# A four-layer graph network on one core: clears on GpSimd behind each gather of the third layer

## The chip, the cores and the metric

The kernel runs on one of the cores of a Trainium2 chip. A core has five engines that run side by side: TensorE (PE in the profile), VectorE (DVE), ScalarE (ACT), GpSimd (POOL) and SyncE (SP). Engines wait for each other through counters, the semaphores. The metric is the device time of one execution in microseconds, the median of three runs: 18546.07 us, with runs from 18542.13 to 18560.46 us. The profile is that of a further execution, taken by the hardware profiler.

## The reference

A graph of 12,500 nodes with 32 features each and 400,000 edges goes through four layers, each followed by a sum with its input and a layer norm:

```
x = layernorm(x + L0(x, edge_attr_3))      # Gaussian weights per edge, sum by node, 32x32 product
x = layernorm(x + L1(x, edge_weight, ...)) # tensor product per edge, sum by node
x = layernorm(x + L2(x, edge_attr_32))     # the third layer, below
x = layernorm(x + L3(x, src, dst))         # ten rounds of a normalised sum by node
```

The third layer, which the change touches, is

```
e_feat = concatenate([x[src], x[dst], edge_attr], axis=-1)   # 96 numbers per edge
h = relu(e_feat @ W1 + b1)                                   # 64
v = h @ W2 + b2                                              # 32
x_cand = segment_max(v, dst)                                 # maximum by node
out = maximum(x_cand, x)
```

## The kernel before, in words

The edges are sorted by their target node and cut into G = 196 groups of 2048 edges (128 partitions x T = 16). Each layer is a stage of its own, with a program for each engine. In the profile the first layer runs from about 630 to 6,550 us, the second from 6,600 to 12,430, the third from 12,915 to 17,820, the fourth from 18,000 to the end.

The third layer's program starts at line 2450. For each group its engines do this:

- **POOL** (function `gathers`, lines 2527 to 2539) fetches the source rows x[src]. One gather is an indirect DMA (line 2537): it takes 128 row numbers from `s_i`, one for each partition, and brings 128 rows of 32 words from the table `d_tab` into one slot of `xg[n]`. A group is 16 such gathers (CH x ST = 4 x 4), one behind the other. There are DEEP = 4 buffers `xg`, used in turn, so POOL may be up to four groups ahead. Before a group it waits for `fxg{n}` (line 2532), the word that buffer n has been read; behind the wait stands the wait's decrement (line 2533, under which the profile books the idle time). At a group that begins a block of four, it also waits for the row numbers (`li{d}`, loaded by SP).
- **PE** waits in `features` (line 2671) until all 16 gathers of the group have landed (`gx{n}`), turns them into `xp` by four transposes (line 2674) and says so on semaphore `xp`.
- **ACT** waits for that (line 2620) and copies `xp` to `XT` (line 2621).
- **PE**, in `step` (line 2685), waits for `XT` (line 2691), frees the gathers' buffer by `fxg` (line 2692) and multiplies `XT` and `U` by W1 into `hb` (lines 2695 and 2696). ACT applies the ReLU (line 2616), PE multiplies by W2 into `vp` (line 2681), DVE takes the running maximum by node (`scan`, line 1180), PE turns the result back (line 1195), ACT copies it and stores it.
- **DVE** also makes `U`, the targets' rows and edge features spread over their edges (line 2574).

Between these, the engines do a share of the fourth layer's preparation: DVE makes one-hot rows (`ol`, line 1021, and `ok`, line 1023), PE multiplies them (`pw`, line 1035), ACT stores the result (line 1050). Nothing plans the order at run time: each engine's program is written out, one block of eight groups as the body of a loop, and only semaphores hold one engine against another. POOL has nothing else to do in this stage than the 196 x 16 = 3136 gathers.

Of the kernel before, what the change touches and what calls it, by code (L numbers as in the profile page):

```python
# [20 lines left out]
P = 128  # L21
# [3 lines left out]
T = 16  # L25
GE = T * P
EP = G * GE
ST = 4
# [124 lines left out]
def gnn_kernel(nc, a, out):  # L153
# [7 lines left out]
    def S(name):  # L161
        if name not in sems:
            keep = name.startswith(lasting)
            sems[name] = spare.pop() if spare and not keep else ctx.enter_context(nc.semaphore(f"{name}_{next(serial)}"))
        return sems[name]
# [15 lines left out]
    def sb(stack, name, shape, dt=F32):  # L181
        made[0] += 1
        return stack.enter_context(nc.sbuf_tensor(f"{name}_{made[0]}", shape, dt))
# [41 lines left out]
    with ctx:  # L225
# [42 lines left out]
        with ExitStack() as st, nc.Block() as block:  # L268
# [7 lines left out]
            @block.sync  # L276
            def _(e):
                e.dma_start(dA[:, :], a["dst_f"][1:EP + 1].rearrange("(p m) -> p m", p=P)).then_inc(S("ld"), 16)
                e.dma_start(dB[:, :], a["dst_f"][0:EP].rearrange("(p m) -> p m", p=P)).then_inc(S("ld"), 16)
                e.dma_start(d_srcf.rearrange("(p m) -> p m", p=P), a["src_f"].rearrange("(p m) -> p m", p=P)  # L280
                            ).then_inc(S("cp"), 16)
                e.dma_start(d_dstf[0:EP].rearrange("(p m) -> p m", p=P), a["dst_f"][0:EP].rearrange("(p m) -> p m", p=P)
                            ).then_inc(S("cp"), 16)
                e.dma_start(d_dstf[EP:EP + 1].rearrange("(a m) -> a m", a=1),
                            a["dst_f"][EP:EP + 1].rearrange("(a m) -> a m", a=1)).then_inc(S("cp"), 16)
                e.wait_ge(S("cp"), 48)
                e.sem_inc(S("cp"), -48)
# [573 lines left out]

        early.close()
        KR = -(-max(k for _, _, k in RUNS) // 2)
        PU = 4
        HEADS = ((0, 2), (2, 8), (8, WPC))
# [105 lines left out]
        def count_buffers(st, runs):  # L971
            kmax = max(n for _, _, n in runs)
            A = {}
            A["iotak"] = sb(st, "iotak", [P, KW], F16)
            A["iotal"] = sb(st, "iotal", [P, P], BF16)
            A["kt"] = [sb(st, f"kt{h}", [P, 3, WPC // 2 * kmax]) for h in range(2)]
            A["ol"] = [sb(st, f"ol{r}", [P, -(-kmax // 2), P], BF16) for r in range(RU)]
            A["ok"] = [sb(st, f"ok{r}", [P, -(-kmax // 2), KW], BF16) for r in range(RU)]
            A["stage"] = [sb(st, f"stage{h}", [P, NB, AC // 8], U16) for h in range(2)]
            return A  # L980
# [4 lines left out]
        def count_start(e, A):  # L985
            if e.engine.name == "Pool":
                e.iota(A["iotak"][:, :], pattern=[[1, KW]], base=0, channel_multiplier=0,
                       allow_small_or_imprecise_dtypes=True)
                e.iota(A["iotal"][:, :], pattern=[[1, P]], base=0, channel_multiplier=0,
                       allow_small_or_imprecise_dtypes=True).then_inc(S("n_iota"), 1)  # L990
            if e.engine.name == "DVE":
                e.wait_ge(S("n_iota"), 1)
                e.sem_inc(S("n_iota"), -1)
            if e.engine.name == "Activation":
                for h in range(2):
                    prime(e, S(f"n_sg{h}"))
                    e.sem_inc(S(f"n_fkt{h}"), 1)
                for r in range(RU):
                    e.sem_inc(S(f"n_fo{r}"), 1)
                e.sem_inc(S("n_fpw"), 2)  # L1000
# [274 lines left out]
        with ExitStack() as st:  # L1275
# [32 lines left out]
            edges = ExitStack()  # L1308
# [586 lines left out]
        with ExitStack() as st:  # L1895
# [24 lines left out]
            edges = ExitStack()  # L1920
# [502 lines left out]
        with ExitStack() as st:  # L2423
# [4 lines left out]
            edges = ExitStack()  # L2428
            st.enter_context(edges)
            s_i = [sb(edges, f"s_i{d}", [P, 4 * T], I32) for d in range(2)]  # L2430
            xg = [sb(edges, f"xg{n}", [P, T, F]) for n in range(DEEP)]
            XT = sb(edges, "XT", [P, SW])
            Wa = sb(edges, "Wa", [P, P])
            ef = [sb(edges, f"ef{d}", [P, 4 * CH, 2, P]) for d in range(2)]
# [15 lines left out]
            with nc.Block() as block:  # L2450
# [70 lines left out]
                @block.gpsimd  # L2521
                def _(e):
                    count_start(e, A)
                    for n in range(DEEP):
                        e.sem_inc(S(f"fxg{n}"), 1)

                    def gathers(r):
                        n, d, w = r % 4, r // 4, r % 4
                        if w == 0:
                            e.wait_ge(S(f"li{d}"), 16)  # L2530
                            e.sem_inc(S(f"li{d}"), -16)
                        e.wait_ge(S(f"fxg{n}"), 1)
                        e.sem_inc(S(f"fxg{n}"), -1)
                        for j in range(CH):
                            for c in range(ST):
                                col = c * T + w * CH + j
                                e.indirect_dma_start(out=xg[n][:, j * ST + c, :], out_offset=None, in_=d_tab,  # L2537
                                                     in_offset=bass.IndirectOffsetOnAxis(ap=s_i[d][:, col:col + 1], axis=0)
                                                     ).then_inc(S(f"gx{n}"), 16)

                    for r in range(4):
                        gathers(r)
                    with e.Fori(0, G // 8) as it:
                        for r in range(8):
                            gathers((r + 4) % 8)
                    for n in range(DEEP):
                        e.wait_ge(S(f"fxg{n}"), 1)
                        e.sem_inc(S(f"fxg{n}"), -1)
                        e.wait_ge(S(f"gx{n}"), G // 4 * 256)
                        e.inc_swdge_sem([S(f"gx{n}")], [G // 4 * 256], mode="sub")  # L2550
# [57 lines left out]
                def _(e):  # L2608
# [9 lines left out]
                    def features():  # L2618
                        e.wait_ge(S("xp"), 1)
                        e.sem_inc(S("xp"), -1)  # L2620
                        e.activation(XT[:, :], xp[:, :], ACT.Copy).then_inc(S("XT"), 1)

# [32 lines left out]
                def _(e):  # L2655
# [29 lines left out]
                    def step(r, q, first=False, last=False):  # L2685
# [3 lines left out]
                        if q == 0:  # L2689
                            e.wait_ge(S("XT"), 1)  # L2690
                            e.sem_inc(S("XT"), -1)  # L2691
                            e.sem_inc(S(f"fxg{r % 4}"), 1)
                        elif r % 4 == 3:
                            e.sem_inc(S(f"fl{r // 4}"), 1)
                        e.matmul(hb[q][:, :], Wbc[:, :], U[k][q][:, :], start=True, stop=False)  # L2695
                        e.matmul(hb[q][:, :], Wa[64 * q:64 * (q + 1), :], XT[64 * q:64 * (q + 1), :], start=False, stop=True
                                 ).then_inc(S("hz"), 1)
# [929 lines left out]
```

## Time and profile before

| | |
|---|---|
| median of three runs | 18546.07 us (18542.13 to 18560.46) |
| the profiled execution, first to last instruction | 20972.7 us |
| POOL busy in the whole span | 11778.5 us (56%) |
| the third layer's gathers on POOL | 3136, 2996.6 us busy |
| idle of POOL ahead of them | 1865.8 us |

The profiled execution's own time is its span, 20972.7 us; it is 2426.6 us longer than the median of the runs without the profiler. A row of a timeline gives start, length, engine, line, operation, and in brackets how long the engine was idle before and what ended that; "issue" means that nothing the profile shows was waited for. POOLq or PEq is that engine's instruction queue, where it waits for semaphores.

### The profile page before, as it was taken

Reading aid. Unit: us, or ns where it says so; the run is one execution under the profiler, and the core shown is the slowest. Engines: PE = TensorE matmul, PEld = TensorE weight load, DVE = VectorE, ACT = ScalarE, POOL = GpSimd, SP = SyncE. Lnnn points to the kernel's source line nnn. Section 1 sums busy time; section 2 is a strip of 40 time slices with the busy share of each in tenths; the row PEclk is TensorE's granted clock in tenths of the full one; section 3 lists DMA queues with packets and bytes.
Section 4 is the critical chain, followed back from the end, with each engine's and each line's share of the span. In section 5 each row is a group of like instructions: output and inputs, shape, how many; then the busy total and the mean of one; then the engine's idle time right before and its main releaser. Section 6 shows DMA issues by size and latency. Waiting matters only on the chain. (4 is left out here: it accounts for less than half of the span.)

```text
span 20972.7 us, 293199 instructions
## 1 busy us (share of the span) xinstructions
PE 13068.2 (62%) x92471; PEld 7362.5 (35%) x92471; DVE 11202.5 (53%) x19689; ACT 3071.4 (15%) x5120; POOL 11778.5 (56%) x10055
## 2 busy tenths in 40 slices
PE   0565555555554676776766652555555555699999
PEld 0344434333333444444444431122222112355554
DVE  2565544444444777777777773333332222567777
ACT  0222222222221111111111110111111111000000
POOL 4788888888886555555555554666666665100000
PEclk6565555555556888888888885666666666799999
DMA  7333333333333222222222213333333343489998
GB/s 276 47 39 37 37 39 39 39 37 37 38 39 46 47 49 47 48 47 47 48 46 48 46 40 35 73 70 72 76 71 71 71 76 63 125 257 293 292 293 267
DMA packets 2998639, 1817.14 MB, mean 87 GB/s; under 512 B 1730466, under 2 KB 2755819, under 8 KB 2979019
## 3 DMA queue, kind: packets, MB, share of 16 engines
q1 hardware_dynamic: 2201756, 1336.87, 25.1%
q0 software_dynamic: 669312, 166.80, 11.3%
q10 hardware_dynamic: 126512, 300.38, 4.1%
q8 instruction: 539, 8.83, 0.2%
q14 instruction: 520, 4.25, 0.1%
HBM read 1474.43 MB, written 392.90 MB: 89 GB/s over the span
## 5 line engine op out<-in xcount | busy, mean ns | idle before, releaser
L2005 POOL DMA_INDIRECT xg<-d_tab,s_i x3136 | 3254.6, 1038 | 2615.5 <-POOLq L1996 1630.7
L2537 POOL DMA_INDIRECT xg<-d_tab,s_i x3136 | 2996.6, 956 | 1865.8 <-issue 954.8
L2265 PE MATMUL pR<-w,H 128*128 128x384 f32 x6272 | 2703.4, 560 | 1407.6 <-PEq L2259 834.5
L1403 POOL DMA_INDIRECT d_acc<-AG,ix x1568 | 2471.5, 1576 | 527.2 <-issue 459.5
L1403 POOL DMA_INDIRECT d_acc<-T,ix x1568 | 2466.3, 1573 | 478.3 <-issue 437.1
L2923 PE MATMUL pacc<-nodes,HB 128*32 128x512 fp8e4 x47040 | 2663.0, 380 | 42.7 <-PEq L2967 42.7
L2574 DVE TENSOR_TENSOR_SCAN U<-mU,U,up 128x512 f32<-128x512 f32 x392 | 501.6, 1280 | 3289.0 <-DVEq L2573 2688.6
L2265 PEld LDWEIGHTS pR<-w,H 128*128 128x128 f32 x6272 | 1225.8, 215 | 2533.1 <-issue 2182.8
L2695 PE MATMUL hb<-U,Wbc 128*128 128x512 f32 x784 | 642.4, 914 | 2204.7 <-PEq L2691 2023.1
L1756 PE MATMUL pm<-ms,eq 128*128 128x32 f32 x6272 | 1366.4, 399 | 890.5 <-PEq L1754 888.8
L2923 PEld LDWEIGHTS pacc<-nodes,HB 128*32 128x32 f16 x47040 | 1261.5, 97 | 1317.1 <-issue 57.1
L1756 PEld LDWEIGHTS pm<-ms,eq 128*128 128x128 f32 x6272 | 1344.1, 330 | 934.8 <-issue 934.4
L1035 PE MATMUL pw<-ok,ol 128*128 128x392 bf16 x4048 | 1303.7, 458 | 319.3 <-PEq L1033 299.3
L1023 DVE TENSOR_SCALAR ok<-iotak,kt 128x392 bf16<-128x392 f16 x4048 | 1372.9, 390 | 0.0
L2892 DVE TENSOR_SCALAR nodes<-packed 128x1792 int32<-128x1792 int32 x840 | 918.0, 1093 | 756.3 <-DVEq L2890 755.3
L2078 DVE TENSOR_TENSOR AG<-pR,FG 128x512 f32<-128x512 f32 x784 | 538.0, 686 | 950.3 <-DVEq L2066 893.7
L2695 PEld LDWEIGHTS hb<-U,Wbc 128*128 128x128 f32 x784 | 191.4, 283 | 2313.3 <-issue 2308.3
L2089 DVE TENSOR_REDUCE Q<-AG 128x64 f32<-128x1024 f32 x784 | 948.3, 1210 | 0.0
L2893 DVE TENSOR_SCALAR nodes<-packed 128x1792 int32<-128x1792 int32 x840 | 912.4, 1086 | 0.0
L1718 PE MATMUL sr<-ids,two 2*128 2x512 bf16 x784 | 411.6, 525 | 798.2 <-PEq L1721 794.9
L2271 PE MATMUL pQ<-PP,ident 128*128 128x128 f32 x6272 | 806.4, 281 | 120.4 <-issue 117.9
L2271 PEld LDWEIGHTS pQ<-PP,ident 128*128 128x128 f32 x6272 | 795.8, 197 | 209.0 <-issue 109.7
(338 smaller groups left out, 17504.3 us busy)
## 6 DMA issues: line engine op xcount, KB each, us to landing
packed<-d_A SPq DMA_DIRECT2D x420, 1792.0 KB
row<-d_m SPq DMA_DIRECT2D x1568, 64.0 KB
xg<-d_tab,s_i POOLq DMA_INDIRECT x6272
wrow<-d_w SPq DMA_DIRECT2D x196, 512.0 KB
d_scan<-so ACTq DMA_DIRECT2D x392, 256.0 KB
d_A<-stage ACTq DMA_DIRECT2D x97, 784.0 KB
d_ea<-in_ea_t ACTq DMA_DIRECT2D x1, 50176.0 KB
d_exp<-T ACTq DMA_DIRECT2D x1, 50176.0 KB, 250.4
```

Of the source, the lines that this page charges most:

```text
L1023: last = e.tensor_scalar(ok[:, i, :], A["iotak"][:, :], kt[:, 2, s + i:s + i + 1], kt[:, 1, s + i:s + i + 1], ALU.is_equal, ALU.mult)
L1035: last = e.matmul(A["pw"][w % 2][:, 0:KW], A["ol"][u % RU][:, i, :], A["ok"][u % RU][:, i, :], start=(u % 2 == 0 and i == 0), stop=(u % 2 ...
L1403: e.indirect_dma_start(out=d_acc[i], out_offset=bass.IndirectOffsetOnAxis(ap=ix[k][:, t:t + 1], axis=0), in_=mo[k][:, t * F:(t + 1) * F], ...
L1756: last = e.matmul(pm[:, t, :], eq[k][:, t, :], ms[:, t % CH * ST + t // CH, :], start=True, stop=True)
L2005: e.indirect_dma_start(out=xg[k][:, t, :], out_offset=None, in_=d_tab, in_offset=bass.IndirectOffsetOnAxis(ap=s_i[n][:, t:t + 1], axis=0)) ...
L2089: e.tensor_reduce(Q[k][:, :, 2 * u:2 * u + 2, :].rearrange("p r t u -> p t r u"), Pr[u % 3].rearrange("p t (r u) c -> p t r u c", u=8), ax ...
L2265: last = e.matmul(pR[u % 2][:, j, 0:384], H[k][:, (2 * u + j) * P:(2 * u + j + 1) * P], w2[:, :], start=True, stop=True)
L2271: last = e.matmul(pQ[:, :, :], ident[:, :], PP[:, :, :, c, :].rearrange("p u t r -> p (u t) r"), start=(c == 0), stop=(c == 15))
L2537: e.indirect_dma_start(out=xg[n][:, j * ST + c, :], out_offset=None, in_=d_tab, in_offset=bass.IndirectOffsetOnAxis(ap=s_i[d][:, col:col + ...
L2892: e.tensor_scalar(low, both, SMALL, None, ALU.bitwise_and)
L2893: e.tensor_scalar(high, both, 4, SMALL, ALU.logical_shift_right, ALU.bitwise_and).then_inc(S(f"un{u}"), 1)
L2923: end = e.matmul(pacc[k][32 * g:32 * (g + 1), :], HB[i][:, b0 + bb, 32 * h:32 * (h + 1)], of, start=(begins and h == 0), stop=(ends and h ...
```

## The change

Behind each gather of the third layer, POOL clears 96 words in every partition of a new tile `pace`, which nothing reads. The tile has two halves of 16 slots; group r uses half r modulo 2, and each of its 16 clears has a slot of its own. Each clear counts up `paced0` or `paced1`. Before a group, POOL waits until the 16 clears of the group two before have been counted; both semaphores begin at 16, so that the first two groups pass. At the end POOL waits for the last clears. The other engines' programs are the same.

```diff
             xg = [sb(edges, f"xg{n}", [P, T, F]) for n in range(DEEP)]
+            pace = sb(edges, "pace", [P, 2, T, 96])
...
                         e.wait_ge(S(f"fxg{n}"), 1)
                         e.sem_inc(S(f"fxg{n}"), -1)
+                        e.wait_ge(S(f"paced{r % 2}"), T)
+                        e.sem_inc(S(f"paced{r % 2}"), -T)
                         for j in range(CH):
                             for c in range(ST):
                                 col = c * T + w * CH + j
                                 e.indirect_dma_start(out=xg[n][:, j * ST + c, :], out_offset=None, in_=d_tab,
                                                      in_offset=bass.IndirectOffsetOnAxis(ap=s_i[d][:, col:col + 1], axis=0)
                                                      ).then_inc(S(f"gx{n}"), 16)
-
+                                e.memset(pace[:, r % 2, j * ST + c, :], 0.0).then_inc(S(f"paced{r % 2}"), 1)
+
+                    for k in range(2):
+                        e.sem_inc(S(f"paced{k}"), T)
                     for r in range(4):
                         gathers(r)
...
+                    for k in range(2):
+                        e.wait_ge(S(f"paced{k}"), T)
+                        e.sem_inc(S(f"paced{k}"), -T)
```

On POOL, before, the body of the loop holds eight groups, of which these are the first four; each row is a run of 16 gathers (`xg_263` to `xg_266` are the four buffers, `s_i_262` the row numbers):

```order
L2537 DMA xg_263<-d_tab,s_i_262 128x32 x16
L2537 DMA xg_264<-d_tab,s_i_262 128x32 x16
L2537 DMA xg_265<-d_tab,s_i_262 128x32 x16
L2537 DMA xg_266<-d_tab,s_i_262 128x32 x16
L2537 DMA xg_263<-d_tab,s_i_261 128x32 x16
```

On POOL, now, at the same place (the gather's line is 2540, the clear's 2543), a group's last gathers and the first of the next:

```order
L2540 DMA xg_263<-d_tab,s_i_261 128x32
L2543 MEMSET pace 128x96
L2540 DMA xg_263<-d_tab,s_i_261 128x32
L2543 MEMSET pace 128x96
L2540 DMA xg_264<-d_tab,s_i_261 128x32
L2543 MEMSET pace 128x96
L2540 DMA xg_264<-d_tab,s_i_261 128x32
L2543 MEMSET pace 128x96
```

No gather changes its place among the gathers; between each two of them, across groups too, there is now one clear.

## Rows read from the trace of the kernel before

**Rows 1.** The page: the span, then its costliest groups of gathers.
```profile
span 20972.7 us, 293199 instructions
...
L2005 POOL DMA_INDIRECT xg<-d_tab,s_i x3136 | 3254.6, 1038 | 2615.5 <-POOLq L1996 1630.7 <-issue 771.7 <-DMA xg<-d_tab,s_i 186.8
L2537 POOL DMA_INDIRECT xg<-d_tab,s_i x3136 | 2996.6, 956 | 1865.8 <-issue 954.8 <-POOLq L2533 910.7 <-PEq L2692 0.3
```
**Rows 2.** Windows: the third layer's gather time, busy us (and instructions) by engine.
```profile
core 0: us, PE busy (x) PEld busy (x) DVE busy (x) ACT busy (x) POOL busy (x), PEclk, DMA share, GB/s
12915.00:17776.00 4861.00, 2588.04 (x6798) 961.97 (x6798) 1408.54 (x2769) 659.23 (x1144) 2996.58 (x3136) 0.68 0.37 72
```
**Rows 3.** Timeline of POOL: the third layer's first two groups.
```profile
12915.76 0.98 POOL L2537 DMA_INDIRECT xg<-d_tab,s_i  x1 [2.49 <-POOLq L2533]
12917.05 0.96 POOL L2537 DMA_INDIRECT xg<-d_tab,s_i  x1 [0.30 <-issue]
...
12935.78 0.94 POOL L2537 DMA_INDIRECT xg<-d_tab,s_i  x1 [0.30 <-issue]
12937.03 0.94 POOL L2537 DMA_INDIRECT xg<-d_tab,s_i  x1 [0.30 <-issue]
```
**Rows 4.** Timeline of all engines, a group and a half in mid-layer.
```profile
15005.42 0.60 PE L2674 MATMUL xp<-ident,xg 128*128 128x128 f32 x4
...
15012.68 0.94 POOL L2537 DMA_INDIRECT xg<-d_tab,s_i  x1 [0.30 <-issue]
...
15016.90 0.60 ACT L2621 ACTIVATE XT<-xp 128x512 f32<-128x512 f32 x1 [13.30 <-ACTq L2620]
...
15017.84 2.04 PE L2695 MATMUL hb<-U,Wbc 128*128 128x512 f32 x2 [11.82 <-PEq L2691]
15018.57 0.94 POOL L2537 DMA_INDIRECT xg<-d_tab,s_i  x1 [4.94 <-POOLq L2533]
...
15033.24 0.60 PE L2674 MATMUL xp<-ident,xg 128*128 128x128 f32 x4
15037.69 0.95 POOL L2537 DMA_INDIRECT xg<-d_tab,s_i  x1 [0.30 <-issue]
15041.50 0.60 ACT L2621 ACTIVATE XT<-xp 128x512 f32<-128x512 f32 x1 [11.85 <-ACTq L2620]
...
15043.12 0.94 POOL L2537 DMA_INDIRECT xg<-d_tab,s_i  x1 [4.48 <-POOLq L2533]
```
**Rows 5.** Timeline of POOL's last gather and of ACT's last copies to XT.
```profile
17774.67 0.94 POOL L2537 DMA_INDIRECT xg<-d_tab,s_i  x1 [0.30 <-issue]
...
17778.74 0.60 ACT L2621 ACTIVATE XT<-xp 128x512 f32<-128x512 f32 x1 [13.35 <-ACTq L2620]
17793.79 0.60 ACT L2621 ACTIVATE XT<-xp 128x512 f32<-128x512 f32 x1 [2.55 <-ACTq L2620]
17806.23 0.60 ACT L2621 ACTIVATE XT<-xp 128x512 f32<-128x512 f32 x1 [4.26 <-ACTq L2620]
17816.33 0.60 ACT L2621 ACTIVATE XT<-xp 128x512 f32<-128x512 f32 x1 [1.93 <-ACTq L2620]
```
**Rows 6.** Groups on POOL: clears of 1 and of 128 words per partition.
```profile
L3617 POOL MEMSET const-float32-0.0<- 128x1 f32 x1 | 0.1, 103 | 0.3 <-issue 0.3
L311 POOL MEMSET ones<- 128x128 f32 x1 | 0.2, 204 | 0.2 <-POOLq L310 0.2
```
**Rows 7.** Timeline of POOL: a gather and what follows; an operation and the gather behind.
```profile
258.45 0.94 POOL L641 DMA_INDIRECT oh<-d_dstf,at_i  x1 [0.30 <-issue]
259.42 0.22 POOL L648 TENSOR_SCALAR_AFFINE_SELECT pick<-pick 48x32 bf16<-48x32 bf16 x1
...
12491.02 0.23 POOL L894 IOTA iotal<- 128x128 bf16 x1
12491.41 0.95 POOL L1088 DMA_INDIRECT AG<-d_scan,endi  x1 [0.16 <-issue]
```
**Rows 8.** Timeline of POOL at the start: clears back to back.
```profile
0.82 2.71 POOL L302 MEMSET T<- 128x3136 f32 x1 [0.29 <-POOLq L3617]
3.47 0.75 POOL L303 MEMSET zt<- 128x784 f32 x1
4.16 0.21 POOL L304 MEMSET ident<- 128x128 f32 x1
```
**Rows 9.** Timeline: a short POOL operation beside a long one of DVE.
```profile
265.70 6.69 DVE L535 TENSOR_TENSOR below<-oh,nodes 128x6272 bf16<-128x6272 int32 x1 [119.43 <-DMA oh<-d_dstf,at_i]
...
266.70 5.76 POOL L648 TENSOR_SCALAR_AFFINE_SELECT pick<-pick 48x32 bf16<-48x32 bf16 x1 [3.29 <-issue]
272.69 0.20 POOL L648 TENSOR_SCALAR_AFFINE_SELECT pick<-pick 48x32 bf16<-48x32 bf16 x1 [0.23 <-POOLq L652]
```
**Rows 10.** Groups in 13000 to 17500 us: DVE's most frequent operation.
```profile
L1023 DVE TENSOR_SCALAR ok<-iotak,kt 128x392 bf16<-128x392 f16 x1346 | 460.5, 381 | 0.0
```

## The prediction

> **What bounds the kernel now.** I read the page's costliest groups first. The third layer's 3136 gathers on POOL stand there with 2996.6 us of work and 1865.8 us of idle time ahead of them, of which 954.8 us is "issue" (POOL waits for nothing that the profile shows) and 910.7 us is the wait at L2533 for a buffer to be given back [rows 1]. Together that is 4862 us, the whole length of the stage, or 24.81 us for each of the 196 groups. In the windows view no other engine comes near it: PE is busy for 2588 of 4861 us, DVE for 1409, ACT for 659 [rows 2]. So the stage goes at the pace of a ring: POOL, the engines that use up its buffers, and POOL again.
>
> POOL's own part is read from its timeline. A gather takes 0.94 us, the next begins 0.30 us later [rows 3]; from the first gather of group 0 (12915.76) to the first of group 1 (12935.78) 20.0 us pass. By the groups' sums it is (2996.6 + 954.8)/196 = 20.16 us. The other 4.65 us (910.7/196) is the wait.
>
> What ends that wait is the odd thing in this trace. In mid-layer PE transposes `xp` at 15005.42, but ACT copies it to `XT` only at 15016.90, having idled for 13.30 us on just this word. The copy comes 3.3 us after POOL's last gather of a group has ended (15012.68 + 0.94). Only then does PE go on (15017.84), and POOL gets its buffer at 15018.57. A group later it is the same: transposes at 15033.24, POOL's last gather ends at 15038.64, the copy comes at 15041.50, and POOL's next gather at 15043.12 [rows 4]. At the stage's end, when POOL has no gathers left, the copies follow each other after 15.05, 12.44 and 10.10 us [rows 5]. So PE, DVE and ACT need 10 to 15 us for a group, less than POOL's 20; but while POOL issues gathers, PE's word to ACT seems to be held.
>
> Is that so in the runs without the profiler too? The profiled span is 20972.7 us, 2426.6 us above the median. The second layer's gathers have a wait of the same size, 1630.7 us at L1996; with the 910.7 us of L2533 that is 2541 us, about the whole excess [rows 1]. I take it that the held words belong mostly to the profiled execution, and that in the timed runs POOL runs from group to group without a pause: 196 × 20.16 = 3951 us for the stage instead of 4862. Either way, each tenth of a microsecond that a gather's step gains in length lies on the path: without the hold POOL alone sets the period, with it POOL's 16 steps and the hold stand one behind the other.
>
> In a sentence that the sum does without: the Trainium skill, "NOTIFIC — the notification-queue block", sections 3 (Interfaces) and 7.1 (Overflow), states that the block which writes an engine's records can push back when its internal queue is full, and can stall an engine by it. That would make the waits of [rows 4] the profiler's own; no row here shows the records' path.
>
> **The change part by part.** On PE, DVE, ACT and SP nothing changes. No gather changes its place. Three things are added on POOL.
>
> The wait for the clears of two groups before: these ended a whole group (20 us) earlier, so it passes. It and its decrement are two instructions per group, 196 times, beside the wait and decrement for `fxg`; I price them at nothing. What would be queued behind them if they did not pass is the group's 16 gathers, and all engines behind those. The waits behind the loop stand once, after the last gather, where 40 us of work by the others still follow (17775.6 to 17816.9) [rows 5].
>
> The room: `pace` has 12 KB per partition; that moves other tiles and no time.
>
> The 3136 clears: the size 128 × 96 does not stand in this trace. The nearest are 103 ns for one word and 204 ns for 128 words per partition [rows 6]; between them 96 words give 103 + 95/127 × 101 = 179 ns. What surrounds it counts too. Gather behind gather, POOL idles for 0.30 us. When something else stands behind a gather it begins after 0.03 us (258.45 + 0.94 = 259.39, next start 259.42), and a gather behind another operation begins 0.16 us after its end (12491.02 + 0.23 = 12491.25, next start 12491.41) [rows 7]. A step then has 0.94 + 0.03 + 0.18 + 0.16 = 1.31 us instead of 0.94 + 0.30 = 1.24: net 0.07 us. Thus much of the clear would lie in time that is now "issue".
>
> To this comes what a clear waits for DVE. A short POOL operation that ran beside a long one of DVE took 5.76 us, and the same 0.20 us once DVE was done [rows 9]. In this stage DVE's most frequent operation, `ok`, takes 381 ns and is busy for 460.5 of 4500 us, a tenth [rows 10]; if every clear that meets one waited for half of it, that is 0.10 × 0.19 = 0.02 us. I take 0.01, since I don't know that `ok` holds POOL at all.
>
> So the step grows by 0.08 us and the stage by 3136 × 0.08 = 251 us. Bounds: from below 0, if the 0.30 us swallow the clear whole (0.18 < 0.30). From above 0.179 × 3136 = 561 us, if the gap stays 0.30 us and the clear comes on top. Starts of clears that follow each other (0.82, 3.47 and 4.16 us) give another price: 2.65 us for 3136 words and 0.69 us for 784 [rows 8], thus 0.83 ns a word and 0.04 us besides, 0.117 us for 96 words; on top of an unchanged gap that is 367 us, between the ends. I stay with 251, since [rows 7] show this very sequence, gather, other operation, gather.
>
> A sentence apart: the Trainium skill, "Perfetto Trace Analysis", section "GPSIMD Engine Instruction", says that spans of this engine are not to be trusted and that one should go by the spacing of starts. By that rule the gap of 0.30 us is partly the gather's own work, nothing is covered, and the sum is the 367 us just worked out; [rows 8] agree in that the recorded 2.71 us overlap the next start by 0.06 us.
>
> Against the profile's own time the sum is 20972.7 + 251 = 21,224 us, if the hold stays as it is; against the median 18546 + 251 = 18,797 us. The 2427 us between these two are, as said, put down to the waits on L1996 and L2533.
>
> **The rivals.**
>
> *The clears come wholly on top* (0.20). Then 18546 + 561 = 19,107 us. For it: a gather's recorded end need not be the end of POOL's work on it. Against it: the 0.16 us before the gather in [rows 7].
>
> *The clears let PE's words through: faster* (0.27). If the hold of [rows 4] is there in the timed runs too, and comes from POOL issuing gathers back to back, then a pause behind each gather may end it. POOL then runs through at 16 × (1.26 + 0.08) = 21.4 us a group, against up to 24.81. At most that gives 3.4 × 196 = 670 us, 17,876 us. It decides from a hold of 16 × 0.08 = 1.28 us a group on; at half of the hold, 2.3 us, it gives (2.3 − 1.28) × 196 = 200 us, 18,346 us. For it: that `XT` follows the end of POOL's run in both groups of [rows 4]. Against it: the profile's excess leaves little of the hold for the timed runs (2541 of waits, 2427 of excess). In the profile alone this could happen as well, and the span fall while the median rises.
>
> *No change* (0.11). The gap swallows the clears, or a hold that shortens by 1.28 us pays for them, or a bound other than POOL hides them: 18,546 us. For it: 0.18 us is less than 0.30. Against it: the gap of 0.16 us that remains behind an operation.
>
> That the change doesn't do what it says is hardly possible: 3136 clears stand in POOL's order, one behind each gather.
>
> **How the numbers follow.** Forecast, clear partly covered: 18,797 us, chance 0.42, by itself from 18,640 to 18,950 (net 0.03 to 0.13 us a step). With it 0.20 for the clear on top, 0.11 for no change, 0.27 for faster. The range shall hold 8 in 10: it goes up to 19,130, past the whole price of 561 us, and down to 18,150, which takes in a hold of up to 3.3 us a group that is lifted, (3.3 − 1.28) × 196 = 396. Left out are a lift of nearly the whole hold and waits that no row shows. A measurement of this kernel tells 0.2%, 37 us, from no change. Slower is the forecast and the first rival, 0.62, less a little for a sum that ends within 37 us: 0.61; same 0.11 and that little, 0.12; faster 0.27.
>
> **What would show it.** In the changed kernel's timeline of POOL: from gather to gather 1.33 us instead of 1.25, with a clear of about 0.18 us between and gaps of 0.03 and 0.16 us. If it is 1.43, the clear is on top; if 1.25, it is hidden. The idle time at the `fxg` wait shows the hold: about 4.6 us a group if the clears do nothing to it, near none if they lift it; then `XT` no longer follows the end of POOL's run. The first, second and fourth layers' groups must keep their sums. The prediction is wrong if the median falls while the steps lengthen: then the timed runs had the hold too. It is also wrong if the steps lengthen by 0.08 us and the median doesn't move: then POOL did not set the pace.

## The result, and the profile after

The changed kernel takes 18757.15 us (18741.16 to 18762.31, 4 runs) against 18550.56 us (18542.13 to 18560.46, 4 runs) of the kernel before: 207 us more, a ratio of 1.0107 with an interval of 1.0094 to 1.0119. A second timing gave 1.0111 (1.0095 to 1.0126). The prediction was 18,797 us, 251 us more.

Side by side, the two first profiles mislead. The page of the changed kernel has a span of 18739.0 us, which is shorter than the 20972.7 us of [rows 1] by 2234 us, although the kernel is slower. The profile of before was taken in an execution that was disturbed; none of the executions that were timed was like it (the longest of the kernel before took 18564.83 us). So the kernel before was profiled once more (experiment "before_again" below: span 18562.7 us), and that is the profile to set beside the one after.

Here are the POOL groups of the changed kernel that answer to [rows 1]; the columns are as there:

```profile
span 18739.0 us, 296535 instructions
...
L2005 POOL DMA_INDIRECT xg<-d_tab,s_i x3136 | 3283.4, 1047 | 1276.2 <-DMA xg<-d_tab,s_i 651.7 <-issue 531.4 <-POOLq L1996 85.1
L2540 POOL DMA_INDIRECT xg<-d_tab,s_i x3136 | 3019.5, 963 | 517.8 <-issue 484.1 <-POOLq L2536 28.0 <-POOLq L2534 4.9
...
L2543 POOL MEMSET pace<- 128x96 f32 x3136 | 623.0, 199 | 1.7
```

And those of the undisturbed profile of before:

```profile
span 18562.7 us, 293199 instructions
...
L2005 POOL DMA_INDIRECT xg<-d_tab,s_i x3136 | 3313.6, 1057 | 1269.3 <-DMA xg<-d_tab,s_i 640.4 <-issue 526.9 <-POOLq L1996 89.6
L2537 POOL DMA_INDIRECT xg<-d_tab,s_i x3136 | 3002.7, 957 | 958.4 <-issue 903.5 <-POOLq L2533 54.6 <-POOLq L2548 0.3
```

In the third layer the gathers themselves are alike (963 and 957 ns). The idle time ahead of them falls from 958.4 to 517.8 us, by 441 us; the clears bring 623.0 us. The difference of these two is 182 us, and the gathers' own work adds 17 us, 199 us together by recorded lengths, which overlap a little. The wait for a buffer is gone in both: 54.6 us at L2533 is 0.32 us at each of 172 groups, about the usual gap. The second layer, whose code is the same, has work and idle time of 4560 us in the changed kernel's profile and 4583 us in this one, and neither has the 1630.7 us of L1996.

The step, from POOL's timeline of the changed kernel in mid-layer:

```profile
15004.28 0.95 POOL L2540 DMA_INDIRECT xg<-d_tab,s_i  x1 [0.17 <-issue]
15005.23 0.20 POOL L2543 MEMSET pace<- 128x96 f32 x1
15005.59 0.95 POOL L2540 DMA_INDIRECT xg<-d_tab,s_i  x1 [0.17 <-issue]
15006.53 0.20 POOL L2543 MEMSET pace<- 128x96 f32 x1
15006.90 0.95 POOL L2540 DMA_INDIRECT xg<-d_tab,s_i  x1 [0.16 <-issue]
```

The same place in the undisturbed profile of before:

```profile
15005.80 0.95 POOL L2537 DMA_INDIRECT xg<-d_tab,s_i  x1 [0.30 <-issue]
15007.05 0.94 POOL L2537 DMA_INDIRECT xg<-d_tab,s_i  x1 [0.30 <-issue]
15008.30 0.95 POOL L2537 DMA_INDIRECT xg<-d_tab,s_i  x1 [0.30 <-issue]
```

From gather to gather it is 1.31 us now (15005.59 − 15004.28) and was 1.25. The clear begins right at the gather's end, and the next gather begins 0.16 us behind it. So of 0.20 us of clear, 0.14 lie in what was gap.

What other engines saw of it stands in the views of the gathers' lines, first after, then before: the stretch from the first to the last gather, and who waited for the gathers (kind, tile, line, us, times). The three numbers in front are the shortest, median and longest gather in ns.

```profile
L2540 POOL DMA_INDIRECT xg<-d_tab,s_i x3136: 950/951/1213, 11465.6 to 15615.7; - x196
...
  PE xp L2683: 1148.5, 194
```
```profile
L2537 POOL DMA_INDIRECT xg<-d_tab,s_i x3136: 941/947/1409, 11483.1 to 15440.8; - x196
...
  PE xp L2674: 984.6, 193
```

The stretch of the gathers goes from 3957.7 to 4150.1 us, by 192 us. The spans of these two executions differ by less, 176 us, since the third layer's gathers began 17.5 us earlier in the changed kernel's. Two profiles can be set against each other to some 15 us only: among the four traces below with an unchanged step (before_again, word1, waits_only, two_clears) the stretch is between 3943 and 3958 us. Within that, the 192 us account for the 207, whose interval goes from 174 to 221 us. PE waits for the landing of the gathers in nearly every group, and by 164 us more than before. That is what a stage looks like in which POOL sets the pace: the others idle on it, it does not idle on them. The last layer is nearly untouched. In the windows view (columns as in [rows 2]) its final 2862 us hold 2787.85 us of PE before, in the first fence, and 2787.21 after, in the second:

```profile
15700.00:18562.00 2862.00, 2787.85 (x51424) 1432.08 (x51412) 1985.63 (x2141) 47.44 (x78) 0.00 (x0) 0.99 0.90 274
```
```profile
15877.00:18739.00 2862.00, 2787.21 (x51416) 1432.28 (x51408) 1986.29 (x2141) 47.40 (x78) 0.00 (x0) 0.99 0.90 274
```

### The profile page after: what moved, and what is told of

It is laid out like the page before. It is cut to its first block and busy times, and to the rows that moved or that the text cites. A ratio compares the mean times of both kernels' runs of the same rounds, so it can differ in the third digit from the quotient of the medians.

```text
span 18739.0 us, 296535 instructions
## 1 busy us (share of the span) xinstructions
PE 12769.7 (68%) x92471; PEld 7193.8 (38%) x92471; DVE 11171.0 (60%) x19689; ACT 3071.9 (16%) x5120; POOL 12486.0 (67%) x13191
## 5 line engine op out<-in xcount | busy, mean ns | idle before, releaser
L2540 POOL DMA_INDIRECT xg<-d_tab,s_i x3136 | 3019.5, 963 | 517.8 <-issue 484.1
L2265 PE MATMUL pR<-w,H 128*128 128x384 f32 x6272 | 2437.8, 514 | 809.7 <-PEq L2259 803.3
L2265 PEld LDWEIGHTS pR<-w,H 128*128 128x128 f32 x6272 | 1102.6, 195 | 1793.7 <-issue 1391.0
L2683 PE MATMUL xp<-ident,xg 128*128 128x128 f32 x784 | 210.4, 423 | 1148.5 <-DMA xg<-d_tab,s_i 1148.5
L1035 PEld LDWEIGHTS pw<-ok,ol 128*128 128x128 bf16 x4048 | 441.6, 128 | 1082.7 <-issue 1029.0
L1453 DVE TENSOR_SCALAR ix<-nf,dump 128x16 int32<-128x16 f32 x196 | 49.3, 252 | 1323.5 <-DVEq L1452 1323.5
L1556 DVE TENSOR_TENSOR eq<-sr,sf 128x512 f32<-128x512 f32 x784 | 536.8, 685 | 498.0 <-DVEq L1555 498.0
```

The lines of the kernel that those rows point to most:

```text
L1035: last = e.matmul(A["pw"][w % 2][:, 0:KW], A["ol"][u % RU][:, i, :], A["ok"][u % RU][:, i, :], start=(u % 2 == 0 and i == 0), stop=(u % 2 ...
L2265: last = e.matmul(pR[u % 2][:, j, 0:384], H[k][:, (2 * u + j) * P:(2 * u + j + 1) * P], w2[:, :], start=True, stop=True)
```

## The experiments

**The kernel before once more** (before_again; no edit).

> The kernel before once more, to see whether the held words belong to it. Step theory (POOL sets the pace of the third layer, a step is from gather to gather): no hold in an execution as short as the timed ones; span near 18,546 us, steps of 1.25 us without a wait for the buffer, the third layer's gathers over 196 x 16 x 1.25 = about 3,930 us, against 4,151 us in the changed kernel. Rival (the hold belongs to gathers that follow each other without a pause): the wait at the buffer shows again, 4 to 5 us a group, and the span is far above 18,546 us, near 20,970 us.

Measured: span 18562.7 us; 18538.0 against 18531.07 us, ratio 1.0002 (0.9993 to 1.0011). Steps of 1.25 us, no wait at the buffer, and the gathers' stretch is 3957.7 us. In the disturbed profile the same stretch was 4859 us (12915.8 to 17774.7), and that of the second layer 5795 us against 4505 us: 901 and 1290 us, 2191 of the 2410 us by which the spans differ. The rows of PE's transposes and ACT's copy show that nothing is held here:

```profile
15020.76 1.08 PE L2674 MATMUL xp<-ident,xg 128*128 128x128 f32 x4 [3.35 <-DMA xg<-d_tab,s_i]
15020.81 0.95 POOL L2537 DMA_INDIRECT xg<-d_tab,s_i  x1 [0.30 <-issue]
15021.96 0.60 ACT L2621 ACTIVATE XT<-xp 128x512 f32<-128x512 f32 x1 [6.37 <-ACTq L2620]
```

ACT copies 0.12 us after the transposes end (15021.84), in the midst of POOL's gathers; in [rows 4] it copied 10.9 and 7.7 us after they had ended. Counted over all 196 groups, the copy came 10.4 us (median) behind the transposes in the disturbed trace, 181 times in a pause of POOL of over 1 us; here it comes 0.12 us (median) behind them, never in such a pause. So gathers without a pause do not by themselves hold PE's words. Step theory holds; the rival falls.

**Clears of one word** (word1).

```diff
-e.memset(pace[:, r % 2, j * ST + c, :], 0.0)
+e.memset(pace[:, r % 2, j * ST + c, 0:1], 0.0)
```

> Clears of 1 word per partition instead of 96, all else as in the changed kernel. Step theory: step = gather 0.951 + clear 0.10 + gap 0.165 = 1.216 us, less than the 1.25 us of two gathers without a clear; 3136 x (1.216 - 1.31) = -295 us against the changed kernel, near 18,460 us, thus some 90 us less than before. Rival (each added instruction has a fixed price, 207/3136 = 0.066 us, whatever its size): 18,757 us as with 96 words. Rival (the clears cost by their words alone, in the way of other engines): 18,546 us, as before.

Measured: 18533.78 against 18531.07 us, ratio 1.0001 (0.9992 to 1.0010). No change: the step theory had expected 90 us less, and its number is wrong. The timeline shows why:

```profile
14002.07 0.94 POOL L2540 DMA_INDIRECT xg<-d_tab,s_i  x1 [0.19 <-issue]
14003.01 0.12 POOL L2543 MEMSET pace<- 128x1 f32 x1
14003.32 0.95 POOL L2540 DMA_INDIRECT xg<-d_tab,s_i  x1 [0.19 <-issue]
```

The step stays 1.25 us. Behind the small clear the gap is 0.19 us instead of 0.165. There is a floor: in this trace no gather of the layer begins less than 0.30 us after the end of the last, though a clear stands between. That the clear can hide in the gap is shown; that it could shorten the step is refuted. A fixed price per added instruction falls too. The price by words alone stays open.

**The waits alone** (waits_only): the memset is left out and the semaphore counted up at the end of each group.

```diff
-                                e.memset(pace[:, r % 2, j * ST + c, :], 0.0).then_inc(S(f"paced{r % 2}"), 1)
+                        e.sem_inc(S(f"paced{r % 2}"), T)
```

> The waits of the change without the clears: POOL counts the semaphore up itself at the end of each group. Step theory: one more semaphore instruction and a wait per group, all within what stands between groups anyhow: 18,546 us to 18,580 us. Rival (the 207 us come from the waits for the clears, or from the loop's greater length of code): up to 18,757 us.

Measured: 18534.95 against 18531.07 us, ratio 1.0001 (0.9992 to 1.0010). The waits cost nothing that can be measured, and neither does the room, since `pace` is still laid out: from 15 us less to 19 us more by the interval. The 207 us belong to the clears.

**One clear per group** (group_end): the memset stands behind the loop over the gathers.

```diff
+                        e.memset(pace[:, r % 2, :, :], 0.0).then_inc(S(f"paced{r % 2}"), T)
```

> The same words in one clear of 16 x 96 words behind the group's last gather instead of 16 clears. Step theory: per group one clear of 1536 words, 0.04 + 1536 x 0.83 ns = 1.31 us by the start-to-start rate, with the gap 0.30 before the next gather cut to 0.165: 196 x (1.31 - 0.135) = +230 us, 18,776 us. Fixed price per clear: 196 x 0.066 = +13 us, 18,559 us. If POOL had slack between groups it would be near 18,546 us too.

Measured: 18780.61 against 18531.07 us, +250 us, ratio 1.0132 (1.0117 to 1.0148). A group's boundary in the timeline:

```profile
14016.02 0.94 POOL L2540 DMA_INDIRECT xg<-d_tab,s_i  x1 [0.30 <-issue]
14016.96 1.40 POOL L2543 MEMSET pace<- 128x1536 f32 x1
14018.52 0.95 POOL L2540 DMA_INDIRECT xg<-d_tab,s_i  x1 [0.17 <-issue]
```

The clear takes 1.40 us, of which 0.30 − 0.17 is covered: 1.27 × 196 = 249 us. The expected 230 us had the clear at 1.31. The stretch of the gathers grew by 239 us (11465.1 to 15661.8). POOL has no slack between its groups. A fixed price per clear falls again.

**Two clears of one word** (two_clears) behind each gather, with the counts doubled:

```diff
+e.memset(pace[:, r % 2, j * ST + c, 0:1], 0.0).then_inc(S(f"paced{r % 2}"), 1)
+e.memset(pace[:, r % 2, j * ST + c, 1:2], 0.0).then_inc(S(f"paced{r % 2}"), 1)
```

> Two clears of 1 word each behind each gather. Floor theory (a gather holds the next one off for 1.25 us from start to start; what POOL does in between costs only what goes beyond that, with 0.165 us ahead of the next gather): step = 0.95 + 0.115 + 0.115 + 0.165 = 1.345 us, +0.095 us a step, 3136 x 0.095 = +298 us on the kernel before, near 18,830 us. Rival (only the words cost, an instruction's fixed part is hidden): 2 words, +5 us, near 18,536 us.

Measured: 18530.3 against 18535.87 us, ratio 0.9998 (0.9989 to 1.0007). The number of the floor theory is wrong, that of the words alone fits. The timeline shows that the sum was made wrongly:

```profile
14000.85 0.94 POOL L2540 DMA_INDIRECT xg<-d_tab,s_i  x1 [0.16 <-issue]
14001.79 0.12 POOL L2543 MEMSET pace<- 128x1 f32 x1
14001.82 0.12 POOL L2544 MEMSET pace<- 128x1 f32 x1
14002.10 0.94 POOL L2540 DMA_INDIRECT xg<-d_tab,s_i  x1 [0.16 <-issue]
```

The two clears are recorded with 0.12 us each, but start 0.03 us apart. The second adds 0.03, not 0.12: 0.94 + 0.03 + 0.12 + 0.16 = 1.25 us, still the floor. That amends the theory and doesn't yet decide it, since words alone say the same.

**Clears of 48 words** (word48).

```diff
-e.memset(pace[:, r % 2, j * ST + c, :], 0.0)
+e.memset(pace[:, r % 2, j * ST + c, 0:48], 0.0)
```

> Clears of 48 words. Floor theory: a clear of 0.153 us (between 0.115 for 1 and 0.192 for 96 words), step = 0.95 + 0.153 + 0.165 = 1.268 us, +0.018 us, 3136 x 0.018 = +56 us, near 18,590 us. Rival (cost by the word): 47/95 of the changed kernel's +226 us, +112 us, near 18,640 us.

Measured: 18597.91 against 18535.87 us, +62 us, ratio 1.0035 (1.0022 to 1.0049), that is +41 to +91 us. The price by the word, +112, lies outside; the floor's +56 inside. Half the words cost less than a third: the first ones are covered. The step is 1.27 us:

```profile
14002.31 0.95 POOL L2540 DMA_INDIRECT xg<-d_tab,s_i  x1 [0.16 <-issue]
14003.25 0.16 POOL L2543 MEMSET pace<- 128x48 f32 x1
14003.58 0.95 POOL L2540 DMA_INDIRECT xg<-d_tab,s_i  x1 [0.16 <-issue]
```

The clear's median is 0.157 us, so the sum is 0.95 + 0.157 + 0.16 = 1.267, where 1.268 was worked out before the run:

```profile
L2543 POOL MEMSET pace<- x3136: 152/157/337, 11468.4 to 15475.8; 128x48 f32 x196
```

**Four clears of one word** (four_clears), with the counts times four; the edit as for two.

> Four clears of 1 word each behind each gather. Amended floor theory (a step is the gather's 0.945 us and then the longer of 0.30 us and the clears with 0.16 us behind them; clears behind each other start 0.03 us apart, as in the kernel with two): 0.945 + 3 x 0.03 + 0.118 + 0.16 = 1.313 us, 0.063 us over 1.25, 3136 x 0.063 = +198 us, near 18,735 us. Rival (only words cost): 4 words, +5 us, near 18,540 us. Rival (clears cost their recorded length, 0.118 us each): 0.945 + 0.472 + 0.16 = 1.577 us, +1,025 us, near 19,560 us.

Measured: 18715.46 against 18535.14 us, +180 us, ratio 1.0098 (1.0082 to 1.0115). Two clears are free, four cost nearly as much as one of 96 words. The amended floor theory's +198 us lies within the interval (+152 to +213 us). Words alone (+5 us) fall, and so does the recorded length of the clears (+1,025 us):

```profile
13999.42 0.94 POOL L2540 DMA_INDIRECT xg<-d_tab,s_i  x1 [0.15 <-issue]
14000.37 0.11 POOL L2543 MEMSET pace<- 128x1 f32 x1
14000.40 0.11 POOL L2544 MEMSET pace<- 128x1 f32 x1
14000.42 0.11 POOL L2545 MEMSET pace<- 128x1 f32 x1
14000.45 0.11 POOL L2546 MEMSET pace<- 128x1 f32 x1
14000.72 1.17 POOL L2540 DMA_INDIRECT xg<-d_tab,s_i  x1 [0.15 <-issue]
```

From the gather's end to the end of the last clear are 0.20 us, behind it 0.15 to 0.16, and the step is 1.30 us (worked out: 1.313).

**Gathers of 64 rows** (half_rows), in the kernel before; this kernel leaves out half of the source rows, so it prices a step and is no faster way to the same result:

```diff
-e.indirect_dma_start(out=xg[n][:, j * ST + c, :], ... ap=s_i[d][:, col:col + 1] ...
+e.indirect_dma_start(out=xg[n][0:64, j * ST + c, :], ... ap=s_i[d][0:64, col:col + 1] ...
```

> The kernel before, whose gathers of the third layer fetch only 64 of the 128 rows (the other 64 partitions of the buffers keep what stands there). It tells whether time also falls when POOL's step gets shorter. Theory that POOL alone sets the pace: the stage falls by 3136 times what the step loses, until the chain of PE, ACT and DVE, 10 to 15 us a group, is the longest; for a step of 0.75 us 196 x (20 - 15) = 980 us less, near 17,550 us. If a gather's time doesn't hang on its rows the step stays 1.25 us and the time 18,531 us; then it says nothing on the pace. Rival (another bound lies just below POOL, a group at 20 us): the steps get shorter, waits for the buffer appear, and the time stays near 18,531 us.

Measured: 18420.4 against 18535.87 us, −115 us, ratio 0.9938 (0.9925 to 0.9952). A gather of half the rows is only 5% shorter (median 900 ns instead of 947), so the large fall that was sketched did not come. But what the gathers lost came through: they were busy for 131 us less (2871.8 instead of 3002.7; the medians give 0.047 us × 3136 = 147), their stretch went from 3957.7 to 3827.4 us, by 130, and the wait for a buffer did not grow:

```profile
L2537 POOL DMA_INDIRECT xg<-d_tab,s_i x3136 | 2871.8, 916 | 958.8 <-issue 903.9 <-POOLq L2533 54.5 <-POOLq L2548 0.3
```
```profile
L2537 POOL DMA_INDIRECT xg<-d_tab,s_i x3136: 893/900/1373, 11469.1 to 15296.5; - x196
```

The 115 us of the timing have an interval from 89 to 139. So the pace is POOL's also for shorter steps, by at least this much.

**The changed kernel again** (after_again; no edit), timed with the three of two clears, 48 words and half the rows.

> The changed kernel again, beside the kernels it is compared with: +207 us on the kernel before as first measured; steps of 1.31 us, 3136 x 0.06 = +188 us by the steps of the two traces.

Measured: 18735.33 against 18535.87 us, +199 us, between the 188 us of the steps and the 207 us of the first timing, with an interval from 176 to 234 us; the gathers' stretch is 4150.6 us (11457.9 to 15608.5), within 0.5 us of the first profile.

## Why the prediction was right, step by step

**POOL sets the pace of the third layer**: right, shown from both sides. Clears lengthen the time by as much as they lengthen POOL's step (group_end +250 us, where 249 were added; word48 +62, where its gathers' stretch, 11467.4 to 15474.9, grew by 50), and a shorter gather shortens it (half_rows: −115 us, where POOL's work fell by 131).

**The hold belongs to the profiled execution**: right, and it was the choice on which the sign hung. None of the ten later profiles shows it (the changed kernel's two, the kernel before's second and those of the seven other experiments). The step to it, the excess of 2427 us against 2541 us of waits, held; the excess is not those waits alone, as 219 of the 2410 us lie outside the two stretches of gathers. What disturbed that execution stays open. That the block which writes the profile's records pushed back, as the Trainium skill ("NOTIFIC — the notification-queue block", sections 3 and 7.1) allows, is not shown by any run here. But that trace, and it alone, lacks records: it keeps 154,129 changes of semaphores, the second profile of the same kernel 315,907, with 293,199 instructions in both, and the other nine traces between 316,330 and 328,697. So the recording was disturbed together with the execution; which of the two came first is not shown.

**The clear partly covered, 0.07 us a step**: right in its form, 1.31 us a step as worked out, and nearly in its size. Term by term, in medians over the stage: the gap ahead of the clear was put at 0.03 us and is 0.00 (−94 us over 3136 steps); the clear was put at 0.179 us and is 0.192 in its median (+41 us); the 0.16 us ahead of the next gather is 0.165 (+16 us). The gather was put at 0.94 us in both steps; it is 0.95, and the step without clears 1.25 instead of 1.24, which cancels. Together with 0.007 us for the next term: 0.065 us instead of 0.08, some 200 us; the stretch of gathers grew by 192, the time by 207 and 199 us in its two timings, and 251 were forecast. The oversized term is the gap ahead of the clear, carried over from another operation [rows 7]; the two undersized ones made up for part of it.

**The wait for DVE, 0.01 us**: about right, with some luck, since no row gave its size. The clears' mean is 199 ns, their least and their median are both 192 (the first two of the three numbers):

```profile
L2543 POOL MEMSET pace<- x3136: 192/192/378, 11466.6 to 15616.6; 128x96 f32 x196
```

That is 7 ns a clear and 21 us in all, the most that waits of the clears can have cost. The 437 clears that overlap an `ok` in time hold 13 of the 21 us, 29 ns each, the other 2699 hold 3 ns each. So nothing here is like the 5.76 us of [rows 9].

**The waits for the clears at nothing**: right (waits_only: 1.0001).

**The rivals.** The clear wholly on top (19,107 us) is refuted by the 207 us and by the gap of 0.16 us; the sum of 367 us, by starts of clears with an unchanged gap [rows 8], by the same. That much of the Trainium skill's rule ("Perfetto Trace Analysis", section "GPSIMD Engine Instruction") was needed all the same: not for one clear behind a gather, whose recorded length held, but for clears behind each other, whose spans overlap (0.12 us recorded, 0.03 us from start to start). The faster rival needed the hold in the timed executions; it isn't there (its most was put at 670 us; 24.81 − 21.44 = 3.37 us a group give 661). No change would have been right for a clear of up to about 28 words: 0.95 + x + 0.16 = 1.25 leaves 0.14 us, and between 0.12 us for 1 word and 0.157 us for 48 that is where x lies, by an estimate along a straight line between these two; this size was not run.

No version here that fetches all rows is faster than the kernel before by more than the noise. Clears of one or two words are free and give nothing; the floor of 1.25 us a gather is what would have to fall, and half the rows take only 0.05 us off it.

## What to carry to other kernels

Before a stage is judged by a profile, set the profiled span beside the timed runs: where it is much longer (here 13%), look for waits that make up the difference, price the change with them and without, and profile once more. Where an engine sets the pace by a row of like instructions, read the step from start to start, and price an insertion as the longer of the gap that stands there anyhow and the inserted work with the gap behind it. Here an idle gap of 0.30 us had room for some 0.14 us of POOL's other work, and no more.

## What was not expected of the hardware

- After a gather (0.95 us) the next one starts no sooner than 0.30 us later, also with a 1-word clear in between (step 1.25 us). A clear starts right at the gather's end, and a gather follows it by 0.15 to 0.19 us (medians of the seven traces with clears). So clears of up to some 0.14 us are free there (1 word, 0.12 us: ratio 1.0001), and what goes beyond costs in full (48 words: +62 us, 96 words: +207 us).
- Clears of 1 word behind each other are recorded with 0.11 to 0.12 us each but start 0.03 us apart; four of them added 180 us and not the 1,025 us of their recorded lengths.
- Half the rows of a gather (64 of 128) save 47 ns of 947.
- One profiled execution of eleven took 13% longer. POOL waited for buffers in two layers (1630.7 and 910.7 us); in the third, ACT saw PE's word only in POOL's pauses in 181 of 196 groups. No timed execution and no other profile was like it, and its trace keeps half the changes of semaphores that the second profile of the kernel has. Its cause is open.
